# Attention and FFN layer on one core: the second of sixteen pipelined tiles gets the usual placement of its FFN pieces in place of its own

## The reference

```
x = x + 0.5 * ffn(layernorm(x))
x = x + attention(layernorm(x))      # 16 heads of 8 features
x = x + 0.5 * ffn(layernorm(x))
ffn(h):       s2 * (relu(2 * s1 * (relu(2 * s0 * ([h, -h] @ w0)) @ w1)) @ w2), weights +1 or -1,
              widths 128 -> 512 -> 512 -> 128
attention(x): q, k, v = projections of x with biases; softmax(q k^T / sqrt(8)) v per head;
              then layernorm(context + x) * gamma + beta
```

## Time and profile before

| | us |
|---|---|
| median of 3 runs | 707.1 |
| lowest and highest | 705.83, 707.26 |
| the profiled execution | 705.83 |
| its span, first to last instruction | 704.0 |
| busy: TensorE, VectorE, GpSimd, ScalarE | 659.1, 618.1, 475.7, 474.6 |
| mean granted TensorE clock | 0.998 of 2.4 GHz |

### The profile page before, as it was taken

The page is one execution under the profiler, slowest core; times in us unless marked ns, Lnnn a source line. Parts: engine busy times, 40 slices in busy tenths (PEclk is TensorE's granted clock), DMA queues, the critical chain, the costliest instruction groups (busy, mean ns, idle before and its releaser), DMA issues. The chain is left out here.

```text
span 704.0 us, 18134 instructions
## 1 busy us (share of the span) xinstructions
PE 659.1 (94%) x7042; PEld 305.6 (43%) x7042; DVE 618.1 (88%) x1229; ACT 474.6 (67%) x641; POOL 475.7 (68%) x790
## 2 busy tenths in 40 slices
PE   6888888999999999999999999999999998888887
PEld 2434242444444444444434444444444444343446
DVE  6778888999999999989999989989999998888766
ACT  3436766777677777777776777777777776776743
POOL 5556549697787868787786869777786876254330
PEclk9999999999999999999999999999999999999999
DMA  3132322222322322221222322222222231120000
GB/s 86 31 65 62 69 62 54 74 55 40 91 52 62 70 76 66 56 77 37 77 59 73 69 74 55 54 82 46 69 64 77 50 63 40 30 72 10 21 1 31
DMA packets 90963, 40.49 MB, mean 58 GB/s; under 512 B 65792, under 2 KB 90880, under 8 KB 90880
## 3 DMA queue, kind: packets, MB, share of 16 engines
q1 hardware_dynamic: 89264, 38.63, 22.4%
q10 hardware_dynamic: 1616, 0.72, 0.4%
HBM read 5.05 MB, written 4.19 MB: 13 GB/s over the span
## 5 line engine op out<-in xcount | busy, mean ns | idle before, releaser
L1323 ACT ACTIVATE probs<-ps_t,score_scale 128x1024 f32<-128x1024 f32 x252 | 280.4, 1113 | 107.9 <-PE ps_t L1015 105.2
L1669 DVE TENSOR_REDUCE row_max<-ps_s 128x4 f32<-128x1024 f32 x256 | 311.1, 1215 | 18.4 <-PE ps_s L1002 17.7
L1541 DVE SCALAR_TENSOR_TENSOR ffn_lo<-ps_z,ffn_hi 128x512 f16<-128x512 f32 x232 | 157.9, 685 | 34.8 <-ACT ffn_hi L1281 31.1
L877 PE MATMUL ps_z<-ffn_hi,w 128*128 128x512 f16 x464 | 177.1, 382 | 1.0 <-DVE ffn_lo L1541 0.8
L878 PE MATMUL ps_z<-ffn_lo,w 128*128 128x512 f16 x464 | 175.9, 379 | 0.0
L1281 ACT ACTIVATE ffn_hi<-ps_z 128x512 f16<-128x512 f32 x232 | 137.8, 595 | 42.3 <-PE ps_z L867 19.0
L1054 PE MATMUL ps_c<-probs,v_cols 128*32 128x256 f32 x2048 | 132.5, 386 | 2.5 <-ACT ctx_t L1333 2.2
L1002 PE MATMUL ps_s<-k_rows,q_rows 32*128 32x256 f16 x1024 | 100.2, 273 | 23.5 <-DVE row_max L1669 19.0
L1015 PE MATMUL ps_t<-q_rows,k_rows 32*128 32x256 f16 x992 | 97.1, 273 | 0.0
L1054 PEld LDWEIGHTS ps_c<-probs,v_cols 128*32 128x32 f32 x2048 | 56.9, 110 | 57.2 <-issue 28.4
L1002 PEld LDWEIGHTS ps_s<-k_rows,q_rows 32*128 32x128 f16 x1024 | 29.0, 92 | 121.4 <-DVE row_max L1669 86.8
(11 more groups left out here) (222 smaller groups left out, 1029.3 us busy)
## 6 DMA issues: line engine op xcount, KB each, us to landing
x<-L_attn_x SPq DMA_DIRECT2D x16, 256.0 KB, 2.9
q_rows<-q_hi SPq DMA_DIRECT2D x32, 128.0 KB, 2.1
k_rows<-k_hi SPq DMA_DIRECT2D x31, 128.0 KB, 2.1
y<-x SPq DMA_DIRECT2D x15, 256.0 KB, 2.2
q_rows<-no_max SPq DMA_DIRECT2D x16, 128.0 KB, 2.1
q_rows<-q_lo SPq DMA_DIRECT2D x16, 128.0 KB, 2.1
k_rows<-k_lo SPq DMA_DIRECT2D x15, 128.0 KB, 2.1
max_cols<-max_wide SPq DMA_TRANSPOSE x63, 2.3
```

What stands on the lines that cost most here:

```text
L877: pe.matmul(o[:], w, ffn_hi[:, 1 + k, :], start=(k == 0), stop=False)
L1323: a_.activation(probs[n % PROBS][:, j:j + 2, :], o[:], ACT.Exp, scale=score_scale[:, 0:1]).then_inc(s_exp, 1)
L1541: v.scalar_tensor_tensor(out=ffn_lo[:, use, :], in0=z_bank(f, use)[:], scalar=0.0, in1=ffn_hi[:, use, :], op0=ALU.max, op1=ALU.subtract).t ...
L1669: v.tensor_reduce(row_max[hb % 2][:].rearrange("p (a l) e -> p l a e", a=2)[:, j:j + 2, :, g % 2], ps_s[:].rearrange("p l (a k) -> p l a k ...
```

## The change

- Iteration 1 loses its pace and the tables ending in `_ONE`, except `AT_STATS_B_ONE`, which becomes `((8, 8, 10, 10), 11)`. It uses `AT`, `AT_CONTEXT`, `AT_STATS_TAIL` and `AT_STATS_PREP`. Its FFN lies in steps 0 to 15, and V moves from step 27 to 29. Steps 16 to 31 have no FFN.
- In steps 22, 26, 28 and 30 of iteration 1 TensorE does 3, 4, 4 and 4 warm-up matmuls, behind a wait for the FFN banks.
- The rows of the FFN of tile 4 are normalised on GpSimd in iteration 1 right after maxima group 0, and transposed on SyncE there, ahead of group 1; the attention residual and context base of tile 2 come after maxima group 1.
- On SyncE in iteration 0 the seven spreads go out together after K, and the transpose of maxima group 2 follows them, directly ahead of its placing.
- `max_wide` is cleared among the constants, and its semaphore goes.

```
-PACE_ONE = {1: 1, 3: 2, 5: 3, 7: 4, 8: 5, 9: 6, 10: 7, 17: 8, 21: 9, 23: 10, 24: 11, 25: 12, 26: 14, 28: 15}
-AT_ONE = {"Q": 11, "K": 13, "CT0": 15, "CT1": 22, "V": 27}
-AT_CONTEXT_ONE = {0: (0,), 2: (1,), 4: (2,), 6: (3,), 16: (4,), 18: (5,), 19: (6,), 20: (7,)}
+WARM_ONE = {22: 3, 26: 4, 28: 4, 30: 4}
-AT_STATS_B_ONE, AT_STATS_PREP_ONE = ((15, 15, 20, 20), 22), ((30, 30, 31, 31), None)
+AT_STATS_B_ONE = ((8, 8, 10, 10), 11)
-AT_STATS_TAIL_ONE = (20, 26)
...
-        self.at = (AT_OWN_LAST if own_contexts else AT_ZERO if not prev else AT_ONE if self.first
-                   else AT_ALONE if pace else AT)
+        self.at = AT_OWN_LAST if own_contexts else AT_ZERO if not prev else AT_ALONE if pace else AT
...
-                Iteration(1, 1, ffn_b=first_ffn(3), next_b=first_ffn(4), misc_base=7, pace=PACE_ONE)]
+                Iteration(1, 1, ffn_b=first_ffn(3), next_b=first_ffn(4), misc_base=7)]
...
             # SyncE
-                if it.stats_a and by_dma(it.ffn_a):
+                if it.first and it.prev:
+                    turn_ffn(it.next_b)
+                elif it.stats_a and by_dma(it.ffn_a):
                     turn_ffn(it.ffn_a)
...
                     turn_max(t, 1)
                     place_max(t, par, 1)
-                    sp.wait_ge(m_free, it.misc["Q"] + 1)
-                    spread(1 - par, 0, Q_SPREADS)
-                    turn_max(t, 2)
                     sp.wait_ge(m_free, it.misc["K"] + 1)
-                    spread(1 - par, Q_SPREADS, SPREADS)
-                    place_max(t, par, 2)
+                    spread(1 - par, 0, SPREADS)
...
-                if it.cur and it.prev:
+                if it.cur:
                     turn_max(t, 2)
                     place_max(t, par, 2)
-                if it.next_b is not None:
+                if it.next_b is not None and (not it.first or not it.prev):
                     turn_ffn(it.next_b)
...
             # GpSimd
             g.memset(xn_scale[:], XN_SCALE)
+            g.memset(max_wide[:], 0.0)
...
             ffn_rows_norm(first_ffn(2), x0[0])
-            g.memset(max_wide[:], 0.0).then_inc(s_mzero, 1)
-            pool.wait_ge(s_mzero, 1)
...
                     att_norm(t + 1, 1 - par)
+                elif it.first:
+                    ffn_rows_norm(it.next_b, x0[1 - par])
                 elif it.stats_a and not alone:
...
-                elif it.prep and not alone:
+                elif it.prep and not alone and not it.first:
                     att_residual(t + 1, 1 - par)
                     context_base(t, par)
                 if it.prev:
                     tail_y(t - 1, 0, 1 - par, it.misc["CT0"])
                 if not it.own_contexts:
                     split_max(t, 1)
+                if it.first and it.prev:
+                    att_residual(t + 1, 1 - par)
+                    context_base(t, par)
...
-                next_rows = it.next_b is not None
+                next_rows = it.next_b is not None and (not it.first or not it.prev)
...
             # TensorE
                         warm(WARM_ZERO[s], ps_c[:])
+                    elif it is head[1] and s in WARM_ONE:
+                        pe.wait_ge(z_free, z_before(it.next_b) - 1)
+                        warm(WARM_ONE[s], z_bank(it.next_b, 1)[:])
```

More of the change, by code:

```diff
@@ L280, in macaron_layer @@
         m_full, m_hi, m_free = sem("misc_full"), sem("misc_hi_made"), sem("misc_free")
-        s_mzero = sem("max_wide_zeroed")
         s_mcols = sem("max_cols_landed")
@@ L397, in at_tails @@
         def at_tails(it):
-            return (AT_STATS_TAIL_ONE if it.first else AT_STATS_TAIL_EARLY if it.own_contexts else AT_STATS_TAIL_BEFORE if it.last_full else AT_STATS_TAIL_ALONE if it.pace and it.prev
+            return (AT_STATS_TAIL_EARLY if it.own_contexts else AT_STATS_TAIL_BEFORE if it.last_full else AT_STATS_TAIL_ALONE if it.pace and it.prev
                     else AT_STATS_TAIL)
@@ L410, in at_stats_prep @@
         def at_stats_prep(it):
-            return AT_STATS_PREP_ZERO if not it.prev else AT_STATS_PREP_ONE if it.first else AT_STATS_PREP_BEFORE if it.last_full else AT_STATS_PREP
+            return AT_STATS_PREP_ZERO if not it.prev else AT_STATS_PREP_BEFORE if it.last_full else AT_STATS_PREP
         def ffn_work(it, s):
@@ L438, in contexts @@
                 return it.t, it.par, (AT_CONTEXT_OWN.index(s),)
-            when = AT_CONTEXT_ONE if it.first else AT_CONTEXT_EARLY if it.own_contexts else AT_CONTEXT
+            when = AT_CONTEXT_EARLY if it.own_contexts else AT_CONTEXT
             return it.t - 1, 1 - it.par, when.get(s, ()) if it.prev else ()
```

## The result

| | before | after |
|---|---|---|
| median, us | 707.18 (4 runs) | 710.94 (4 runs) |
| lowest and highest | 705.83, 707.28 | 710.81, 712.21 |
| ratio to before, 95% interval | | 1.0065 (1.0039 to 1.0091) |
| profiled execution, its span | 705.83, 704.0 | 711.88, 710.1 |
| mean granted clock in it | 0.998 | 0.995 |

The change costs 3.8 us by the medians, 0.5%, or 0.65% by the ratio. I had forecast 1.4 us slower (708.5) with a range up to 710.4, so the result lies 0.5 us above the range.

What follows compares the result with a forecast made beforehand. TensorE, busy 94% of the span, was taken to bound most of the kernel. From 705.83 us, + 2.84 late start, - 0.1 iteration 1, - 1.28 iteration 2 gave 707.3, plus 1.3 for the median 708.5; range 705.8 to 710.4.

Steps and rivals of the forecast that it cites:

- a drop as a rival: Start of iteration 1: TensorE's idle gap makes the clock fall, taking back the 1.28 us gain, 709.8 us; chance 0.23.
- the old drop: Start of iteration 2 in the kernel before: clock 0.50 for 3.41 us, costing iteration 2 at most 1.28 us.
- the 2.7 that I had named as speaking against a drop: Ahead of iteration 1: TensorE's gap may be only 2.7 us long if the maxima transpose lands in 2.3.
- Late start of iteration 1: Iteration 1's first scores wait for placed maxima, delayed behind seven spreads, and start at 76.3 instead of 73.44: 2.84 us late.
- First half, 20.29 us: Iteration 1, steps 0 to 15 with all sixteen FFN pieces: TensorE bounds it, as in iteration 3, at 20.29 us.
- Second half, 15.5 us from step 16: Iteration 1 without FFN: scores and row maxima alternate in cycles of 1.74 us, 14.73 plus small extras, 15.5 us.
- the 0.2 of row maximum 11: Iteration 1, second half: 0.2 us for the second context's reciprocal and product, also covering a 0 to 0.5 hold-up.
- the 8.0 of my chain: Iteration 1: maxima of steps 8 to 14 land 8.0 us after step 16; step 24 needs them about 8 us after.
- Iteration 2, - 1.28 us: Iteration 2 loses its slow start and becomes as long as iteration 3, 40.08 instead of 41.36 us: 1.28 us gained.
- The hidden handover: Start of iteration 1: maxima are placed before row maximum 15 frees ps_s, leaving only gains, -1.4 us, 705.7; chance 0.2.
- The third: Iteration 1, second half: FFN transpose holds up step 24's maxima, or tail work costs a cycle, 1.2 us, 709.7; chance 0.1.
- The fourth: Iteration 1, second half: warm-ups fail and the clock falls there, 1.3 us more, 709.8; chance 0.05.

Runs made afterwards that it cites:

- e2: The changed kernel with iteration 1's transpose of the next FFN's rows moved on SyncE's queue to the end of the iteration; 710.21 us, ratio 1.0045.
- e5: The kernel before, with only the change's late transpose and placing of maxima group 2 behind all seven spreads in iteration 0; 710.52 us, ratio 1.0038.
- e1: The changed kernel with SyncE's order of iteration 0 as before: Q spreads, transpose of maxima group 2, K spreads, placing; 707.16 us, ratio 1.0014.
- e4: The changed kernel with 17 instead of 4 warm-up matmuls in step 30 of iteration 0; 710.3 us, ratio 1.0044.
- e3: The changed kernel with the edits of e1 and e2 together; 706.59 us, ratio 1.0002.
- e6: e1 plus, in iteration 1, the placing of maxima group 1 ahead of the four Q spreads on SyncE's queue; 705.79 us, ratio 0.9976.
- e7: e1 without the fifteen warm-up matmuls of iteration 1; 708.71 us, ratio 1.0017.
- e8: e6 plus warm-up matmuls: 4 in step 24 of iteration 1, 2 each in steps 10 and 12 of iteration 0; 704.41 us, ratio 0.9954.
- e9: The kernel before plus warm-up matmuls only, in steps 28 and 30 of iteration 1 and 10 and 12 of iteration 0; 705.12 us, ratio 0.9981.

## Why the prediction was wrong

**The step that failed** is the forecast's assumption that the clock stays up over the gap. I worked out the gap (72.5 to 76.3), named a drop as a rival, and gave it 0.23 and the price of the old drop, 1.3 us; in the sum the drop stood at nothing. In the changed kernel, in e2 and in e5 the clock fell after this gap, in every profile that had it unfilled, and none of the 22 executions of the changed kernel on record had a mean clock over 0.998, where e1 had 1.0 in three of twelve. The gap was 2.94 us, about the 2.7 that I had named as speaking against a drop. The price was 1.6 us: TensorE's first half took 21.94 (76.58 to the scores of step 16 at 98.52) where 20.30 is e1's (74.70 to 95.00). It is more than the old drop's: in the 3.41 us at half clock TensorE was busy for 2.76 us there and for all 3.41 here. The trace of before had shown 0.62 us of work in 3.41 ahead of a fall; the gap I predicted would leave TensorE 3.8 us with none, so the row spoke for the drop and not for either side. The Trainium skill's "TensorE: Matmul & The Clock Gate", Part 1, prices such a time at one half; the trace agrees with that here better than my row did: the estimate from it is 1.7 us for 3.41 us at 0.50, and 1.6 was measured.

**Late start of iteration 1**: the mechanism was right, the size too large. From the last row maximum of iteration 0 to the scores it is 3.29 us (73.29 to 76.58) against 1.32 before (72.12 to 73.44), so 2.0 us instead of 2.84. I took 3.5 us from issue to landing for the transpose from one row of before and put the length down to the number of spreads ahead of it. Behind all seven it was 2.4 us in each of the four profiles with that order (after, e2, e4, e5). Behind the four Q spreads it is 3.1 to 3.5 us in before, e3, e6, e7, e8 and e9, each time with an issue of 1.62 to 2.40 us instead of 1.2, and 2.4 only in e1. So more spreads ahead did not make it longer, the agreement that I had seen between these landings and the order of the queue is not borne out, and why it is long behind the four stays open. A long issue is not the only way either; in before this one was short and its landing took 4.1 us:

```profile
113.16 1.20 SPq L490 DMA_TRANSPOSE max_cols<-max_wide  x1
```
```profile
DMA to landing us min/median/max: 4.1/4.1/4.1
```

My lower bound, a landing of 2.3, gave 1.7, and was nearer.

**First half, 20.29 us**: right, apart from the clock, as e1's 20.30 shows.

**Second half, 15.5 us from step 16**: the cycles were counted rightly. Counted from row maximum 8 to the next iteration's first, they give 15.5 - 1.24 + 0.43 = 14.7, and e6 and e8, where nothing waits at step 24, have 14.72. The changed kernel has 15.86, or 16.65 on TensorE where I forecast 15.5. The difference is the wait at step 24, which I had put inside the 0.2 of row maximum 11: scores at 107.57 instead of 104.53 + 1.74 = 106.27, 1.3 us. About 0.55 of it is there in e1 too: the placed maxima came 8.3 us after step 16 (95.00 to 103.32), not the 8.0 of my chain, and in e6, where step 24 waits for nothing, it starts 7.75 us after step 16, so even 8.0 was too late for it. 0.74 is the long issue of a spread, for which I had no term. The reason that I named for a hold-up, the FFN transpose ahead, was wrong (e6).

**Iteration 2, - 1.28 us**: right, 41.36 in the earlier trace rows became 40.08.

**Sum.** In the head 1.4 us was forecast and 3.4 measured: the clock + 1.6, step 24 and the rest of the second half + 1.2, the late start - 0.9. The 3.76 of the medians lie near the 3.4. That the late start was overestimated by 0.9 us hid a third of what I had missed; that is luck. I had also priced each rival alone, so the range had no room for a drop together with a longer second half.

**The other rivals.** The hidden handover did not come. The third (the maxima of step 24 held up) did, at about its price of 1.2 us but for another reason than named. The fourth, a fall in the second half, is not in the changed kernel's profile but in e3's, e4's and e7's.

## What to carry to other kernels

When a transfer is moved behind others on its queue, find its consumer and work out both the gap that it leaves on TensorE and the clock after the gap: here the move cost 2.0 us of waiting and 1.6 more at 1.2 GHz. A small transfer that opens the next stage (8 KB of maxima) belongs ahead of the large ones that have time; mending that in two places turned a kernel 0.65% slower into one 0.24% faster. Where TensorE idles in short waits, matmuls on a free bank can keep the clock up: here eight more of them cost nothing and took the median from 705.79 to 704.41 us. Their gain shows in how few executions have a low mean clock (1 of 12 under 0.999 instead of 7), not in any one timeline.

## What the runs showed of the hardware

- An issue on SyncE's queue that takes 0.60 us took 1.19, 1.26, 1.34, 1.49, 1.78 or 1.84 us in single cases (e3, e2, after, e1, e7, e4), each a spread among others that follow one another closely, in three of them (after, e7, e4) the second spread of iteration 1. A transpose of maxima behind the four Q spreads of iteration 0 took 1.62 to 2.40 us instead of 1.2 in six of seven profiles. What makes it so was not tried.
- From issue to landing a transpose of maxima mostly took 2.3 to 2.4 us, 3.1 to 3.5 with these long issues, and 4.0 to 4.1 with an issue of 1.2 in single cases (before at 113.16, e1 at 104.19, e6 at 74.11).
- The clock's first rise came 6.3 us after the start in the execution of before, 12.0 and 12.1 in those of the changed kernel and of e1, 6.3 to 8.9 in others, with the first row maximum at 38.91 to 40.28. e1 and e6 have the same work up to there and differ by 1.3 us (40.28 and 38.99).
- Most falls lasted 3.41 us, one in e3 and one in e4 6.83, and that of e7 at 102.6 13.65. The same kernel has a different mean clock from execution to execution: in the twelve of e1 the mean clock was 1.0 in three, 0.998 in five, and 0.995 or 0.990 in four, with spans from 704.3 to 710.6 us.
